# A gated MLP with LoRA adapters on one NeuronCore: the LoRA matmuls of gate and up by two sequences of 128 columns instead of four of 256

## The chip, the core and the metric

One NeuronCore of a Trainium2 chip runs the whole program. The metric is the device time of one execution in microseconds (us); lower is better. Differences between two kernels are told from runs on the same chip.

## What is computed

The input `x` is 64 sequences of 64 tokens with 512 features, all float32. Sequence b uses adapter `idx[b]`, one of 8, with rank 16. The reference, cut to what matters:

```python
def _lora_linear(x, W, A, B, adapter_indices):
    base = jnp.einsum('bsd,df->bsf', x, W)
    Ai = A[adapter_indices]; Bi = B[adapter_indices]
    lora = jnp.einsum('bsr,brf->bsf', jnp.einsum('bsd,bdr->bsr', x, Ai), Bi)
    return base + lora
gate = _lora_linear(x, Wg, Ag, Bg, adapter_indices)        # 512 -> 2048
up = _lora_linear(x, Wu, Au, Bu, adapter_indices)          # 512 -> 2048
h = jax.nn.silu(gate) * up
x = x + _lora_linear(h, Wd, Ad, Bd, adapter_indices)       # 2048 -> 512
x = x + einsum('bct,bcd->bdt', x, weights[adapter_indices])  # 64 x 64 mix of the tokens
```

## The kernel before

float32 products are made of `float32r` matmuls: each operand is split into a high part (a copy into float32r, on ScalarE: `hi`) and a low part (the value minus its high part, on VectorE: `lo`), and high x high, high x low and low x high are summed in PSUM.

**First phase: gate and up.** `GROUPS` = 4 groups of 1024 tokens (16 sequences, `SLOTS`), and in each 16 chunks c of 128 hidden features: 64 steps s. A step computes gate and up of one chunk with seven Strassen-like products (`prod`, L850 to L859, six matmuls of 512 columns each) into PSUM banks RA, RB, RC. The LoRA parts are added into the same banks by four calls of `lora` (L861 to L870) in a step. VectorE and ScalarE combine the banks (`keep_p1`, `make_c11`, `make_u3` and so on), apply the silu, and `store_h` writes h to DRAM. They also split the weights of the next step (`w_hi_raw`, `w_add`, `w_lo_sum`), and near the end of a group the inputs of the next one (`x_add`, `x_hi`, `x_lo`).

**The LoRA of gate and up.** `lora_a` (L873) computes t = x A in plain float32 for four sequences (a quad, 256 columns): the 128 rows of the result are gate and up (2) x four sequences x rank 16. Its stationary operand `aq` is put together on GpSimd by `gather_a`, one copy for each sequence. `t_mask` (VectorE) copies the bank to `t_f` and sets the rows of other sequences to zero; `t_hi` (ScalarE) and `t_lo` (VectorE) write high and low part of gate's t into rows 0 to 63 and 64 to 127 of `t_st[0]`, and of up's t into `t_st[1]`. B, split into high and low by `b_hi` and `b_lo`, is written to DRAM in 8 pieces of two chunks (`store_b`, one DMA), and `gather_b` fetches for each piece and each of the 16 sequences its adapter's rows, twice (rows 0 to 63 and again 64 to 127 of `bq`): 32 DMAs of 64 KB for two steps, all issued by SyncE. `lora` then does for each of two quads a matmul with B's high part and one with its low part: four matmuls of 256 columns in a call, 16 in a step, 1024 in all.

**Order of the work.** It is written out by hand, as one instruction stream for each engine, with semaphores between them. SyncE issues at step s: `load_w(s+2)`, `store_b(s)` for s below 8, half a gather, `store_h(s-1)`, and at c = 2 `load_x` of the next group. In group 0 the pieces of B are split one in each step (`b_hi(s)`, `b_lo(s)` after the second `w_lo_sum`), so a gather can only begin when the piece of its step is stored. TensorE does all of group 0's `lora_a` within step 0, and that of group g+1 in steps 4 to 7 of group g, one quad at the end of each; `t_mask`, `t_hi` and `t_lo` follow in steps 5 to 8. On VectorE `t_mask` stands ahead of `make_c11` and `t_lo` behind it, ahead of `make_u3`, for whose result TensorE waits ahead of the last product of a step (`prod(..., A22, ...)`).

**Second phase: down, and the mixing of tokens.** 16 pairs of 256 tokens; `down` (L955), `turn`, `lora_down`, `mix_tile`. Nothing of it changes.

## Time and profile before

| | us |
|---|---|
| median of 3 runs (1327.96 to 1330.48) | 1329.66 |
| the profiled execution: its time | 1330.62 |
| the profiled execution: its span in the trace | 1328.7 |
| first phase, to about | 862 |

All durations below are of the profiled execution. PE is TensorE's matmuls, PEld its weight loads, DVE VectorE, ACT ScalarE, POOL GpSimd, SP SyncE; SPq is SyncE's issuing of DMAs. The profile's matmuls overlap: one matmul's record reaches over the start of the next, so what a matmul costs in a stream is read from one start to the next, not from its duration.

### The profile page before, as it was taken

How to read it: one execution, taken by the hardware profiler on the slowest of the kernel's cores; microseconds unless marked ns; L12 is line 12 of the kernel's file. 1: busy time of each engine (PE TensorE's matmuls, PEld its weight loads, DVE VectorE, ACT ScalarE, POOL GpSimd, SP SyncE). 2: the span in 40 equal slices, each digit the busy share in tenths (PEclk: the TensorE clock that was granted, in tenths of full speed). 3: DMA queues.
4: the chain of work that ended last, by engine and by line, in shares of the span. 5: the costliest groups of instructions: out<-in, count | busy, mean ns of one | idle time of the engine just before them, and what ended most of it. 6: DMA issues, size and time to landing. Idle time of an engine off the chain costs nothing.

```text
span 1328.7 us, 22783 instructions
## 1 busy us (share of the span) xinstructions
PE 1226.5 (92%) x7072; PEld 1079.6 (81%) x7072; DVE 754.1 (57%) x1341; ACT 500.7 (38%) x951; POOL 96.3 (7%) x190
## 2 busy tenths in 40 slices
PE   3766999989999989999989999989999999999995
PEld 2555778878888878888878888889998999999994
DVE  5434666776666776666776677544334443434341
ACT  3323444454444454444444444443232232322320
POOL 2100110000110000100000000011111111111110
PEclk9778999999999999999989999989999999999998
DMA  3346776567665576665565777375454554455520
GB/s 137 104 145 227 202 211 185 148 196 229 186 168 156 153 206 211 185 176 152 156 201 167 207 209 214 100 235 179 143 149 150 158 162 145 140 156 165 155 62 32
DMA packets 114362, 221.31 MB, mean 167 GB/s; under 512 B 26434, under 2 KB 68546, under 8 KB 114242
## 3 DMA queue, kind: packets, MB, share of 16 engines
q1 hardware_dynamic: 105824, 198.28, 51.2%
q0 software_dynamic: 7552, 19.93, 4.7%
q10 hardware_dynamic: 866, 1.66, 0.3%
q8 instruction: 56, 0.92, 0.3%
q14 instruction: 64, 0.52, 0.1%
HBM read 173.62 MB, written 46.14 MB: 165 GB/s over the span
## 4 chain that ended last, share of the span: by engine, by line
PE 77%; SPq 7%; DVE 5%; issue 4%; ACT 3%; DMA 3%; POOL 0%; ACTq 0%; DVEq 0%
PE ps L856 14%; PE ps L857 14%; PE ps L858 13%; PE ps L868 8%; PE ps L967 5%; PE ps L971 4%; SPq L194 4%; PE ps L975 4%; PE ps L976 4%; PE ps L974 4%; PE ps L969 4%; PE ps L1001 2%; PE ps L885 1%; ACT hh L359 1%; ACT xo_hi L359 1%
## 5 line engine op out<-in xcount | busy, mean ns | idle before, releaser
L856 PE MATMUL ps<-xo_hi,w_hi 128*128 128x512 f32 x896 | 361.2, 403 | 29.0 <-DVE v L657 13.4
L857 PE MATMUL ps<-xo_lo,w_hi 128*128 128x512 f32 x896 | 356.3, 398 | 0.0
L858 PE MATMUL ps<-xo_hi,w_lo 128*128 128x512 f32 x896 | 353.4, 394 | 0.0
L856 PEld LDWEIGHTS ps<-xo_hi,w_hi 128*128 128x128 f32 x896 | 172.2, 192 | 62.0 <-DVE v L657 16.1
L858 PEld LDWEIGHTS ps<-xo_hi,w_lo 128*128 128x128 f32 x896 | 171.2, 191 | 38.4
L868 PEld LDWEIGHTS ps<-t_st,bq 128*128 128x128 f32 x1024 | 158.6, 192 | 53.1 <-DMA bq<-b_dram 32.9
L577 DVE TENSOR_TENSOR hl<-h_raw,hh 128x1024 fp32r<-128x1024 f32 x64 | 78.4, 1226 | 203.1 <-ACT hh L359 203.1
L857 PEld LDWEIGHTS ps<-xo_lo,w_hi 128*128 128x128 f32 x896 | 172.3, 192 | 26.4
L868 PE MATMUL ps<-t_st,bq 128*128 128x256 f32 x1024 | 165.4, 285 | 30.3 <-DMA bq<-b_dram 30.3
L967 PE MATMUL ps<-wd_hl,hh 128*128 128x320 f32 x512 | 167.8, 328 | 6.8 <-DVE hl L577 4.1
L577 DVE TENSOR_TENSOR w_lo<-wsum,w_hi 128x512 fp32r<-128x512 f32 x128 | 88.6, 692 | 145.7 <-ACT w_hi L359 145.7
L971 PE MATMUL ps<-wd_hl,hl 128*128 128x288 f32 x512 | 151.9, 297 | 0.0
L359 ACT ACTIVATE hh<-h_raw 128x1024 fp32r<-128x1024 f32 x64 | 67.6, 1056 | 214.9 <-PE ps L976 208.1
L975 PE MATMUL ps<-wd_hl,hh 128*128 128x256 f32 x512 | 145.1, 283 | 0.0
L976 PE MATMUL ps<-wd_hl,hl 128*128 128x256 f32 x512 | 144.8, 283 | 0.0
L974 PE MATMUL ps<-wd_hl,hh 128*128 128x256 f32 x512 | 144.6, 283 | 0.0
L969 PE MATMUL ps<-wd_hl,hh 128*128 128x256 f32 x512 | 144.4, 282 | 0.0
L967 PEld LDWEIGHTS ps<-wd_hl,hh 128*128 128x128 f32 x512 | 97.9, 191 | 11.0 <-issue 6.5
L969 PEld LDWEIGHTS ps<-wd_hl,hh 128*128 128x128 f32 x512 | 97.7, 191 | 3.6 <-issue 3.6
L974 PEld LDWEIGHTS ps<-wd_hl,hh 128*128 128x128 f32 x512 | 97.6, 191 | 0.0
L976 PEld LDWEIGHTS ps<-wd_hl,hl 128*128 128x128 f32 x512 | 97.3, 190 | 0.0
L971 PEld LDWEIGHTS ps<-wd_hl,hl 128*128 128x128 f32 x512 | 97.1, 190 | 0.0
(65 smaller groups left out, 1434.9 us busy)
## 6 DMA issues: line engine op xcount, KB each, us to landing
bq<-b_dram SPq DMA_DIRECT2D x1024, 64.0 KB, 2.2
raw<-packed SPq DMA_DIRECT2D x64, 512.0 KB, 5.2
h_dram<-h_f SPq DMA_DIRECT2D x64, 512.0 KB, 3.6
h_raw<-h_dram SPq DMA_DIRECT2D x64, 512.0 KB, 4.0
ad_raw<-a_d SPq DMA_DIRECT2D x64, 128.0 KB, 2.7
xs<-x POOLq DMA_DIRECT2D x16, 512.0 KB, 5.0
y_out_dram<-ys POOLq DMA_DIRECT2D x32, 256.0 KB, 3.3
xst<-xg SPq DMA_DIRECT2D x14, 512.0 KB, 6.3
```

What stands on the lines that cost most here:

```text
L359: return act.activation(dst, src, ACT.Copy)
L577: return dve.tensor_tensor(dst, src, hi.bitcast(F32), ALU.subtract)
L856: pe.matmul(bank, st[0], mv[0], start=start and kk == 0, stop=False, skip_group_check=True)
L857: pe.matmul(bank, st[0], mv[1], start=False, stop=False, skip_group_check=True)
L858: m = pe.matmul(bank, st[1], mv[0], start=False, stop=kk == 1, skip_group_check=True)
L868: m = pe.matmul(bank[:, i * QT:(i + 1) * QT], b[:, q, c % PIECE, a:a + P], t_st[u][g % 2][:, q * QT:(q + 1) * QT], start=start and part == ...
L967: pe.matmul(tile[:, 0:HD + 2 * TR], h_hi, w[:, wide[0]:wide[0] + HD + 2 * TR], start=first, stop=False, skip_group_check=True)
L969: pe.matmul(tile[:, plain:plain + HD], h_hi, w[:, LO0:LO0 + HD], start=False, stop=False, skip_group_check=True)
L971: pe.matmul(tile[:, narrow[1]:narrow[1] + HD + TR], h_lo, w[:, narrow[0]:narrow[0] + HD + TR], start=False, stop=False, skip_group_check=True)
L974: pe.matmul(second, h_hi, w[:, HI1:HI1 + HD], start=first, stop=False, skip_group_check=True)
L975: pe.matmul(second, h_hi, w[:, LO1:LO1 + HD], start=False, stop=False, skip_group_check=True)
L976: m = pe.matmul(second, h_lo, w[:, HI1:HI1 + HD], start=False, stop=False, skip_group_check=True)
```

## The change

Eight duos of two sequences (128 columns) take the place of four quads. The four combinations of high and low lie in the 128 rows of one matmul: `bq` has B's high part in rows 0 to 63 and its low part in rows 64 to 127, each with two sequences of 32 rows; every rank row stands twice, and `t_st` has t's high part in the even rows and its low part in the odd ones. So `lora` does one matmul of 128 columns for each of four duos in a call: again 16 in a step and 1024 in all. `lora_a` computes the doubled rows itself (`aq` holds each column twice, its 128 columns are gate and up x two sequences x 16 x 2), in eight duos of 128 columns, at the ends of steps 6 to 13. For a set of four duos (512 columns) `t_mask` makes two masked copies (one signed, one of the low rows), `t_hi` one high part, `t_sum` adds them for gate and for up (64 rows each), and `t_copy` copies them to the other 64 rows. `store_b` writes each piece with four DMAs.

```diff
@@ tiles
-        bq = [... [P, QUADS, PIECE, BC], F32R) ...]
+        bq = [... [P, DUOS, PIECE, WB], F32R) ...]
-        aq = at("aq", 200704, [P, KT * 2, QS, RANK])
+        aq = at("aq", 200704, [P, KT * 2, 2, ROWS])
@@ SyncE: store_b, gather_b
-                sp.dma_start(b_dram[k].rearrange("a r c -> (a r) c"),
-                             b_hl[:, :, :].bitcast(F32).rearrange("p k c -> p (k c)")).then_inc(b_stored, 16)
+                for part in range(2):
+                    for copy in range(2):
+                        sp.dma_start(b_dram[k, part, :, :, copy, :].rearrange("a r (k c) -> (a r) k c", k=PIECE),
+                                     b_hl[:, :, part * WB:(part + 1) * WB].bitcast(F32)).then_inc(b_stored, 16)
...
-                    for half in range(2):
-                        r = half * QR + (b % QS) * RANK
-                        sp.dma_start(bq[n % 2][r:r + RANK, b // QS, :, :]..., b_dram[k, bass.ds(a, 1)]...)
+                    for part in range(2):
+                        r = (part * 2 + b % 2) * ROWS
+                        sp.dma_start(bq[n % 2][r:r + ROWS, b // 2, :, :]..., b_dram[k, part, bass.ds(a, 1)]...)
@@ GpSimd: gather_a
-                    pool.wait_ge(t_done, g * QUADS + q)
-                for s in range(QS):
-                    a = number(pool, g * SLOTS + q * QS + s)
-                    pool.tensor_copy(aq[:, :, s, :], a_all[:, bass.ds(a, 1), :, :]...)
+                    pool.wait_ge(t_done, g * DUOS + q)
+                for k in range(2):
+                    a = number(pool, g * SLOTS + q * 2 + k)
+                    src = a_all[:, bass.ds(a, 1), :, :].rearrange("p a k r -> p (a k) r")
+                    pool.tensor_copy(aq[:, :, k, :].rearrange("p k (r d) -> p k r d", d=2),
+                                     src.unsqueeze(3).to_broadcast([P, KT * 2, RANK, 2])).then_inc(a_gathered, 1)
@@ ScalarE: t_hi is one copy of 128 x 512; new:
+            def t_copy(g, b):
+                ...
+                for u in range(2):
+                    act.wait_ge(t_set, 2 * i + u + 1)
+                    t = t_st[u][g % 2]
+                    a, z = (slice(0, 2 * ROWS), slice(2 * ROWS, P))[::1 - 2 * u]
+                    hi(t[z, cols], t[a, cols].bitcast(F32)).then_inc(t_ready, 1)
@@ ScalarE, step 0: for b in 0, 1
+                t_hi(0, b)
+                x_hi(0, 3 + 2 * b)
+                t_copy(0, b)
+                x_hi(0, 4 + 2 * b)
@@ ScalarE and VectorE, in the loop over the steps
-                if 5 <= c < 9 and g + 1 < GROUPS:
-                    t_mask(g + 1, c - 5)          # t_hi(g + 1, c - 5) on ScalarE
+                if c in (10, 14) and g + 1 < GROUPS:
+                    t_mask(g + 1, c // 14)        # t_hi and t_copy(g + 1, c // 14) on ScalarE
...
                 make_c11(s)
-                if 5 <= c < 9 and g + 1 < GROUPS:
-                    t_lo(g + 1, c - 5)
+                if c in (10, 14) and g + 1 < GROUPS:
+                    t_sum(g + 1, c // 14)
@@ VectorE: new bodies
+                for dst, m in ((t_f[:, :], sign_mask), (t_low[g][:, 0:HALF], low_mask)):
+                    dve.tensor_tensor(dst..., bank, m[:, :].unsqueeze(2).to_broadcast([P, SLOTS // 2, SEQ]), ALU.mult)
...
+                for u in range(2):      # t_sum
+                    r = slice(u * 2 * ROWS, (u + 1) * 2 * ROWS)
+                    dve.tensor_tensor(t_st[u][g % 2][r, cols], t_low[g][r, 0:HALF], t_hi_s[g][r, 0:HALF].bitcast(F32),
+                                      ALU.add).then_inc(t_set, 1)
@@ VectorE, step 0: for b in 0, 1
+                t_mask(0, b)
+                if b == 0:
+                    x_add(0, 3, None)
+                x_lo(0, 3 + 2 * b)
+                t_sum(0, b)
+                x_lo(0, 4 + 2 * b)
@@ TensorE: lora
-                for part in range(2):
-                    for i in range(2):
-                        q = pair * 2 + i
-                        a = part * WB + u * P
-                        m = pe.matmul(bank[:, i * QT:(i + 1) * QT], b[:, q, c % PIECE, a:a + P],
-                                      t_st[u][g % 2][:, q * QT:(q + 1) * QT], ...)
+                for i in range(SD):
+                    q = half * SD + i
+                    m = pe.matmul(bank[:, i * DT:(i + 1) * DT], b[:, q, c % PIECE, u * P:(u + 1) * P],
+                                  t_st[u][g % 2][:, q * DT:(q + 1) * DT], ...)
@@ TensorE: when step 0 of a group may use t, and when lora_a runs
-                    pe.wait_ge(t_lo_done, 2 * QUADS * (g + 1))
+                    pe.wait_ge(t_ready, 2 * SETS * (g + 1))
...
-                if 4 <= c < 8 and g + 1 < GROUPS:
-                    lora_a(g + 1, c - 4)
+                if 6 <= c < 14 and g + 1 < GROUPS:
+                    lora_a(g + 1, c - 6)
```

## Rows read from the trace of the kernel before

**Rows 1.** The page: busy time and share of an engine, then the chain's shares.

```profile
PE 1226.5 (92%) x7072; PEld 1079.6 (81%) x7072; DVE 754.1 (57%) x1341; ACT 500.7 (38%) x951; POOL 96.3 (7%) x190
...
PE 77%; SPq 7%; DVE 5%; issue 4%; ACT 3%; DMA 3%; POOL 0%; ACTq 0%; DVEq 0%
```

**Rows 2.** Busy time by stretch: one undisturbed step, 11.5 us long.

```profile
436.90:448.40 11.50, 11.50 (x61) 9.78 (x60) 8.23 (x15) 4.94 (x8) 0.00 (x0) 1.00 0.76 219
```

**Rows 3.** Groups of instructions by shape: busy us, mean ns, idle before.

```profile
L868 PE MATMUL ps<-t_st,bq 128*128 128x256 f32 x1024 | 165.4, 285 | 30.3 <-DMA bq<-b_dram 30.3
...
L885 PE MATMUL ps<-xst,aq 128*128 128x256 f32 x128 | 35.3, 425 | 12.1 <-POOL aq L288 12.1
```

**Rows 4.** Timeline of TensorE: start us, us, instruction; a `lora` call in its stream.

```profile
442.84 0.64 PE L868 MATMUL ps<-t_st,bq 128*128 128x256 f32 x4
443.31 0.40 PE L856 MATMUL ps<-xo_hi,w_hi 128*128 128x512 f32 x1
```

**Rows 5.** Timeline of TensorE: matmuls of 128 columns, and what follows them.

```profile
902.36 0.31 PE L984 MATMUL ps<-eye_r,td_hl 128*96 128x128 f32 x2
902.51 0.36 PE L967 MATMUL ps<-wd_hl,hh 128*128 128x320 f32 x1
902.71 0.28 PE L969 MATMUL ps<-wd_hl,hh 128*128 128x256 f32 x1
```

**Rows 6.** Timeline of the weight loads in the same stretch.

```profile
902.45 0.19 PEld L967 LDWEIGHTS ps<-wd_hl,hh 128*128 128x128 f32 x1
902.56 0.19 PEld L969 LDWEIGHTS ps<-wd_hl,hh 128*128 128x128 f32 x1
```

**Rows 7.** Timeline of the weight loads: two of 128 columns after a pause.

```profile
873.05 0.19 PEld L967 LDWEIGHTS ps<-wd_hl,hh 128*128 128x128 f32 x1 [0.52 <-DVE hl L577]
873.16 0.19 PEld L969 LDWEIGHTS ps<-wd_hl,hh 128*128 128x128 f32 x1
```

**Rows 8.** Timeline of step 0: `lora_a`, its copies, and the first `lora`.

```profile
20.89 2.35 PE L885 MATMUL ps<-xst,aq 128*128 128x256 f32 x8
...
34.12 3.78 PE L885 MATMUL ps<-xst,aq 128*128 128x256 f32 x8 [3.90 <-POOL aq L288]
...
38.64 0.30 POOL L288 COPY aq<-a_all 128x128 f32 x1 [4.57 <-PE ps L885]
...
41.80 3.78 PE L885 MATMUL ps<-xst,aq 128*128 128x256 f32 x8 [3.90 <-POOL aq L288]
...
49.96 1.22 PE L868 MATMUL ps<-t_st,bq 128*128 128x256 f32 x4 [4.38 <-DMA bq<-b_dram]
```

**Rows 9.** Chain of work between 60 and 190 us: start us, us, what.

```profile
68.89 2.63 DMA b_dram<-b_hl
...
87.00 2.08 DMA bq<-b_dram
...
118.89 5.79 DMA bq<-b_dram
...
152.31 2.10 DMA bq<-b_dram
```

**Rows 10.** SyncE: `load_x`'s four issues; what `gather_b` executes, ns min/median/max.

```profile
107.50 2.47 SPq L166 DMA_DIRECT2D xst<-xg  x4
...
L194 SPq DMA_DIRECT2D bq<-b_dram x159: 315/368/1440, 71.7 to 199.6; - x159
L194 SPq FUSED_REGOPS  x80: 37/37/42, 71.5 to 199.5; - x80
```

**Rows 11.** Timeline of VectorE in step 13 of group 1, and TensorE's last product.

```profile
442.83 0.69 DVE L577 TENSOR_TENSOR w_lo<-wsum,w_hi 128x512 fp32r<-128x512 f32 x1 [1.17 <-ACT w_hi L359]
443.44 0.69 DVE L588 TENSOR_TENSOR xst<-xst,xst 128x512 f32<-128x512 f32 x1
...
444.90 0.69 DVE L657 TENSOR_TENSOR v<-ps,p_s 128x512 f32<-128x512 f32 x1 [0.17 <-PE ps L858]
...
446.53 0.40 PE L856 MATMUL ps<-xo_hi,w_hi 128*128 128x512 f32 x1
```

More of the change, by code:

```diff
@@ L21 @@
 SLOTS = GT // SEQ
-QUADS, QS = 4, 4
-QT, QR = QS * SEQ, QS * RANK
+DUOS, DT = 8, 2 * SEQ
+SETS, SD = 2, DUOS // 2
+QS = 4
 BLK = 2 * HALF
@@ L319, in _ @@
             pool.wait_ge(a_in, 16)
-            for q in range(QUADS):
+            for q in range(DUOS):
                 gather_a(0, q)
@@ L323, in _ @@
             gather_a(1, 0)
-            for k in range(2, 6):
+            for k in range(2, PIECES):
                 load_b(k)
-            gather_a(1, 1)
-            load_b(6)
-            gather_a(1, 2)
-            load_b(7)
-            gather_a(1, 3)
-            for g in range(2, GROUPS):
-                for q in range(QUADS):
+            for g in range(1, GROUPS):
+                for q in range(g == 1, DUOS):
                     gather_a(g, q)
@@ L502, in _ @@
             w_hi_sum(0, 1)
-            for q in range(QUADS):
-                t_hi(0, q)
-                x_hi(0, 3 + q)
-            act.wait_ge(const_in, 48)
+            for b in range(SETS):
+                t_hi(0, b)
+                x_hi(0, 3 + 2 * b)
+                t_copy(0, b)
+                x_hi(0, 4 + 2 * b)
+            act.wait_ge(const_in, 64)
             hi(eye_r[:, :], eye_f[:, :])
@@ L533, in _ @@
                     b_hi(s)
-                if 5 <= c < 9 and g + 1 < GROUPS:
-                    t_hi(g + 1, c - 5)
+                if c in (10, 14) and g + 1 < GROUPS:
+                    t_hi(g + 1, c // 14)
+                    t_copy(g + 1, c // 14)
                 silu_1(s)
@@ L751, in _ @@
             w_lo_sum(0, 1)
-            dve.wait_ge(const_in, 48)
-            for q in range(QUADS):
-                t_mask(0, q)
-                if q == 0:
+            dve.wait_ge(const_in, 64)
+            for b in range(SETS):
+                t_mask(0, b)
+                if b == 0:
                     x_add(0, 3, None)
-                t_lo(0, q)
-                x_lo(0, 3 + q)
+                x_lo(0, 3 + 2 * b)
+                t_sum(0, b)
+                x_lo(0, 4 + 2 * b)
             for s in range(STEPS):
@@ L859, in prod, with lora @@
                 return m
-            def lora(bank, s, u, pair, start):
+            def lora(bank, s, u, half, start):
                 g, c = divmod(s, CH)
                 b = bq[(s // PIECE) % 2]
-                for part in range(2):
-                    for i in range(2):
-                        q = pair * 2 + i
-                        a = part * WB + u * P
-                        m = pe.matmul(bank[:, i * QT:(i + 1) * QT], b[:, q, c % PIECE, a:a + P],
-                                      t_st[u][g % 2][:, q * QT:(q + 1) * QT], start=start and part == i == 0,
-                                      stop=part == i == 1, skip_group_check=True)
+                for i in range(SD):
+                    q = half * SD + i
+                    m = pe.matmul(bank[:, i * DT:(i + 1) * DT], b[:, q, c % PIECE, u * P:(u + 1) * P],
+                                  t_st[u][g % 2][:, q * DT:(q + 1) * DT], start=start and i == 0,
+                                  stop=i == SD - 1, skip_group_check=True)
                 return m
             def lora_a(g, q):
-                i = g * QUADS + q
-                pe.wait_ge(a_gathered, QS * (i + 1))
+                i = g * DUOS + q
+                pe.wait_ge(a_gathered, 2 * (i + 1))
                 if q == 0:
@@ L910, in step @@
                 if s == 0:
-                    for q in range(QUADS):
+                    for q in range(DUOS):
                         lora_a(0, q)
@@ L1060, in by_chunk @@
         return np.asarray(b).reshape(ADAPTERS * RANK, PIECES, PIECE, P)
+    rows = np.arange(P)[:, None]
+    own = rows % (2 * ROWS) // ROWS == np.arange(SLOTS // 2)[None, :] % 2
+    low = rows % 2 == 1
     arrays = {
@@ L1075 @@
         "w1": ar(np.asarray(L1_cond_weights)),
-        "slot_mask": (np.arange(P)[:, None] % QR // RANK == np.arange(QS)[None, :]).astype(np.float32),
+        "slot_mask": ar(np.stack([own * np.where(low, -1.0, 1.0), own * low]).astype(np.float32)),
         "tok_mask": (np.arange(P)[:, None] // SEQ == np.arange(TR)[None, :] // RANK).astype(np.float32),
```

95 lines of the change are left out of this document (50 added, 45 removed).

## The prediction

> **What bounds the kernel now.** I read the shares of the page first. TensorE is busy for 92% of the span and holds 77% of the chain; VectorE has 57% of its own time [rows 1]. Then a stretch of one undisturbed step: TensorE is never idle in its 11.5 us, VectorE works 8.2 us of it, ScalarE 4.9 [rows 2]. So in steady state a nanosecond less of matmul is a nanosecond less of time, as long as VectorE's 3.3 us of slack last. Group 0 is different: in the chain between 60 and 190 us stand the store of a piece of B, SyncE's issues and the landing of `bq` [rows 9], and `lora` waited 30.3 us for `bq` in all [rows 3]. There nothing that TensorE saves counts, and whatever lengthens the way from `b_lo` through `store_b` and `gather_b` does.
>
> I work against the profiled execution's own 1330.6 us (span 1328.7 and 1.9 around it). It lies 0.9 us above the median of the runs shown; I take that off at the end.
>
> **1. The `lora` matmuls: 1024 of 256 columns become 1024 of 128.** What does one cost? Four of 256 take 443.31 - 442.84 = 0.47 us from the first start to the next line's, 118 ns each [rows 4]. Halved columns would give some 60 ns if columns set the pace. But each matmul has its own stationary operand of 128 columns, and the number of weight loads does not change. How long does a load hold its port? After a pause, with nothing ahead to wait for, the second load starts 873.16 - 873.05 = 0.11 us after the first [rows 7]. The trace has one place with short matmuls, the pairs `turn` (128 columns moving, 96 of weights). Behind them the loads for L967 and L969 start at 902.45 and 902.56, again 0.11 apart [rows 6]. And the time is really lost: from the first of the pair to L969 it is 902.71 - 902.36 = 0.35 us [rows 5]. If columns set it, two of 128 would take 0.06 each and the one of 320 columns 0.15, together 0.27; with loads that hold the port for 0.08 (96 columns) and 0.11 (128) it is 0.08 + 0.11 + 0.15 = 0.34, which fits. So a matmul of 128 columns behind a load of 128 columns costs about 0.11 us. I take 111 ns, hence 7 ns less than now for each: 1024 x 0.007 = 7.2 us gained. Bounds: 0 (118 ns as now) and 1024 x 0.058 = 59 us (60 ns).
>
> [...]
>
> **2. `lora_a`.** 32 matmul halves of 256 columns in a group (128 instructions in all [rows 3]) become 64 of 128. They are plain float32, 3.78 us for eight at the low clock, 0.43 us apart [rows 8], and half of that, 0.215, at the high one; half the columns take half again, and 0.11 us is just what a weight load allows. So TensorE's time for them stays: 0 us. Bounds: 0 and, if a float32 weight load were twice as slow, +6.9 us a group outside step 0, three times; I keep that as tail.
>
> **3. Step 0: the chain of duos.** `lora_a` and `gather_a` take turns there, since there is one `aq`. Now: 0.74 us from the end of a quad (34.12 + 3.78 = 37.90) to the first copy (38.64), then the other three copies until 41.80, then 3.78 us of matmuls: 7.7 us four times from 20.89 on [rows 8]. After: two copies in place of four, but each of twice the elements and eight turns instead of four. [...] Seven turns of 3.0 to 3.9 us, mostly at the low clock, from 22.5 on: the last duo is done at about 48.7 (46 to 51.5), against 45.6 now. Behind it stands more than before: a mask of 512 columns (0.69), `t_hi` (0.62), then in both streams the work on `x`: `x_hi(0,5)` 1.06 and `x_lo(0,5)` 1.23, then two sums of 0.69 and the last `t_copy` 0.62: 5.6 us, where now the mask and the split took 1.9. `t_ready` comes at about 54.3. Now the first `lora` starts at 49.96, when `bq` lands [rows 8]; `bq` will land at 51.5 to 53. So +4.4 us (bounds +1.5, where `bq` alone decides, and +7.5).
>
> **4. Group 0: storing and fetching B.** A store is one DMA now, 2.63 us from issue to the next step of the chain [rows 9]. It becomes four. Four DMAs in a row on SyncE took 2.47 us, 0.6 each, single ones 0.37 [rows 10]; three more cost 1.2 to 1.9 us, I take 1.5. [...] In the chain, the pieces for steps 2 and 3 count: `store_b(1)` ahead of the gather for step 2 (+1.5), `store_b(2)` and `store_b(3)` ahead of that for step 4, where SyncE never waited (+3.0), and `store_b(5)` and `store_b(7)` ahead of those for steps 6 and 8 (+1.5 each; the stores of steps 4 and 6 fall into waits of SyncE of over 2.5 us). Together +7.5 us (bounds 5 and 9.5). The fetch stays at 32 DMAs of 64 KB with 32 runs of 2 KB instead of 16 of 4 KB. One address calculation now serves two DMAs: 80 for 160 [rows 10]. The two will read from different parts, so there may be one for each: 16 more of 0.08 us, 1.3 us in each of the first two gathers of the chain and half of it in the next two, 3.9 us. I take 2 of it (0 to 3.9). What hides them now is nothing: TensorE waits there anyway. From step 10 on SyncE has slack, 32 issues of 0.5 us in 23 us.
>
> **5. VectorE in steps 10 and 14.** Now mask and split of a quad are short and lie in steps 5 to 8. In step 13 VectorE runs `w_lo_sum` at 442.83, `x_add` 443.44, `make_c11`, and `make_u3` from 444.90 to 445.59; TensorE needs it at 446.53, so there is 0.9 us of slack, and 0.6 us for each instruction of this size [rows 11]. Steps 10 and 14 have an `x_add` too, and get two masks ahead and two sums behind `make_c11`: `make_u3` starts at 442.83 + 7 x 0.605 = 447.07 in that step's times, is done at 447.76 and TensorE resumes 1.3 us late. Behind it wait `make_c22`, `make_c12`, silu and h, shifted by as much as TensorE itself. Two such steps in three groups: +7.8 us (bounds 4 and 10, the upper with a bit more at step 15, where `x_lo` already fills VectorE). The stalls that go are those of step 8, which takes 12.0 us in group 1 where 11.5 is usual: 0.4 us three times, -1.2. ScalarE's part is 3.7 us a group against 3.4, in its 6 us of slack.
>
> **Sum.** 1330.6 - 7.2 + 4.4 + 7.5 + 2 + 7.8 - 1.2 = 1343.9; less 0.9 for the median: **1343.0 us**, 1.0% slower.
>
> **Rivals.**
> *Columns set the pace (faster).* The load is hidden behind the matmul ahead at any length and a `lora` matmul takes 60 ns: 59 us in place of 7.2, less what falls into waits (3): 1294. For it: in a stream of 256 columns the loads cost nothing visible [rows 4]. Against: rows 5 to 7. It decides the sign as soon as a matmul takes less than about 98 ns (118 less 20 us over 1024). Chance 0.08.
> *A load holds the port 0.085 us only*, as the 96 columns do behind a short matmul [rows 5]: 1024 x 0.033 = 34 us, so 1343.0 - 26.6 = 1316. [...] Chance 0.06.
> *The costs hide and it comes out even.* Stores go out at 0.4 and no address calculation is added (+5), `bq` decides step 0 (+1.5), VectorE catches up (+2), and the matmuls go to 108 ns (-10): 1328 to 1332. Chance 0.07.
> *The long side*: calculations for every DMA, copies slowed by VectorE in step 0, one more stall at the ends of groups: 1343 + 2 + 3 + 2 + 3 to 1353 and up. It is the forecast's upper end; beyond 1356 I give 0.06.
> The forecast's own case, 1333 to 1356, holds 0.73.
>
> The range that leaves out two in ten: 1330 to 1357. A difference of 0.2%, 2.7 us, is about what can be told from none: faster 0.15, the same 0.07, slower 0.78.
>
> **What would show it.** The distance from start to start within a `lora` call: 0.11 us if I am right, 0.06 if columns set it. An undisturbed step of 11.4 us in place of 11.5. The first `lora` at about 54 us, and waiting for ScalarE's copy rather than for `bq`. Waits for `bq` ahead of steps 2, 4, 6 and 8 still there. Two steps of each of the first three groups with TensorE waiting over 1 us for `make_u3`. The prediction is wrong if a `lora` matmul takes less than 98 ns, or if `store_b`'s four DMAs do not lengthen the chain of group 0 and steps 10 and 14 show no stall.

## The result, and the profile after

The changed kernel takes **1357.38 us** (median of 4 runs, 1356.88 to 1358.11), the kernel before 1329.68 beside it: ratio 1.0214, 95% interval 1.0202 to 1.0226, so 27 to 30 us slower. Forecast were 1343.0 us and 1330 to 1357. The sign was right; the loss is twice the 13 us forecast, just outside the range.

The page of the kernel after, against [rows 1]: the same engines work about as long, the span is 27.8 us longer. (Its chain view breaks off half way, with 37% for TensorE, so I don't read it.)

```profile
span 1356.5 us, 23547 instructions
PE 1220.7 (90%) x7200; PEld 1081.4 (80%) x7200; DVE 759.2 (56%) x1325; ACT 501.1 (37%) x943; POOL 97.2 (7%) x190
...
DMA packets 138448, 225.57 MB, mean 166 GB/s; under 512 B 26962, under 2 KB 77266, under 8 KB 138322
```

Busy time can't tell where the rest went, so next the waits of TensorE and of its weight loads: line, what it waited for, us in total, times, longest. Against [rows 3], where `bq` held it for 30.3 us, it is 44.2. The wait for v (`make_u3`) was 13.4 us in 6 places and is 22.6 in 12.

```profile
PE ps L888 <- DMA bq<-b_dram: 44.2, 6, 17.0
...
PEld ps L878 <- DVE v L678: 24.3, 12, 3.4
...
L878 PE MATMUL ps<-xo_hi,w_hi 128*128 128x512 f32 x896 | 371.3, 414 | 38.5 <-DVE v L678 22.6
```

Where in the span? I compare the starts of the first `lora` matmul of each piece of B, read from TensorE's timeline, and the end of group 0:

| | step 0 | 2 | 4 | 6 | 8 | last h of group 0 |
|---|---|---|---|---|---|---|
| before, us | 49.96 | 89.12 | 124.73 | 154.45 | 183.09 | 278.2 |
| after, us | 56.32 | 99.05 | 137.16 | 169.53 | 202.32 | 307.7 |
| difference | +6.4 | +9.9 | +12.4 | +15.1 | +19.2 | +29.5 |

The whole loss arises in group 0. At the last h of groups 1, 2 and 3 the difference is 30.8, 30.4 and 28.3 us: later groups win by the matmuls about what they lose to VectorE. The step from +19.2 to +29.5 can be read off the lengths of the steps in the trace: six duos of 0.89 us in steps 8 to 13 (the quads before stood in steps 4 to 7) are 5.3, the two steps with a wait for v 3.3, and a granted clock of 0.50 for 6.8 us, from 202.1 on, behind the wait of step 8 makes that step 3.2 us longer; less 1.3 by the shorter matmuls and 0.4 for the old stall in step 8.

An undisturbed step of the kernel after is 11.36 us, against [rows 2] 11.5, with TensorE never idle (columns as there):

```profile
590.00:601.36 11.36, 11.36 (x64) 9.83 (x63) 7.04 (x12) 4.94 (x8) 0.73 (x2) 1.00 0.65 198
```

TensorE around a `lora` call, then step 10 of group 2, its wait in brackets:

```profile
631.53 0.56 PE L888 MATMUL ps<-t_st,bq 128*128 128x128 f32 x4
631.93 0.45 PE L878 MATMUL ps<-xo_hi,w_hi 128*128 128x512 f32 x1
632.21 0.40 PE L879 MATMUL ps<-xo_lo,w_hi 128*128 128x512 f32 x1
...
634.72 0.56 PE L888 MATMUL ps<-t_st,bq 128*128 128x128 f32 x4
636.70 0.50 PE L878 MATMUL ps<-xo_hi,w_hi 128*128 128x512 f32 x1 [1.43 <-DVE v L678]
```

The call seems to cost 0.40 us for four, but the matmul behind it is followed after 0.28 where 0.227 is usual: 0.40 + 0.05, some 112 ns each. Within the call the second start comes only 57 ns after the first and the others 113 and 110 ns apart, so the records of the first and of the matmul behind the call seem to begin early, and starts must be read over the whole call and one matmul more. Read so, the kernel before has 120 ns, not 118. The cause of the wait is in VectorE's timeline of the same step, all its instructions from 631 to 636.7:

```profile
631.52 0.69 DVE L593 TENSOR_TENSOR w_lo<-wsum,w_hi 128x512 fp32r<-128x512 f32 x1 [1.13 <-ACT w_hi L365]
632.13 0.68 DVE L654 TENSOR_TENSOR t_f<-ps,sign_mask 128x512 f32<-128x512 f32 x1
632.73 0.68 DVE L654 TENSOR_TENSOR t_low<-ps,low_mask 128x512 f32<-128x512 f32 x1
633.33 0.68 DVE L604 TENSOR_TENSOR xst<-xst,xst 128x512 f32<-128x512 f32 x1
633.93 0.68 DVE L671 TENSOR_TENSOR p_s<-ps,p_s 128x512 f32<-128x512 f32 x1
634.53 1.39 DVE L665 TENSOR_TENSOR t_st<-t_low,t_hi_s 64x512 fp32r<-64x512 f32 x2
635.96 0.69 DVE L678 TENSOR_TENSOR v<-ps,p_s 128x512 f32<-128x512 f32 x1
```

Seven instructions back to back and then `make_u3`, without a pause: just the queue that the forecast counted. Behind a wait of 1.43 us, step 10 and step 14 of a group are each 1.66 us longer than their neighbours (13.91 for 12.25, 13.02 for 11.36).

SyncE's issues in group 0, start and length; against [rows 9], where the store's step in the chain took 2.63 us:

```profile
74.99 1.96 SPq L186 DMA_DIRECT2D b_dram<-b_hl  x4
81.19 16.20 SPq L203 DMA_DIRECT2D bq<-b_dram  x32
```

From the first store to the first fetch it is 6.20 us; before it was 2.78 at this place. Of these, 1.96 are the four issues and 4.2 the rest of the landing. By the DMA queues' records a store was 512 KB in 128 packets of 4 KB (166 ns each, 1.3 us for each of the 16 DMA engines) and is 1 MB in 1024 packets of 1 KB (47 ns each, 3.0 us for each). At later pieces, where SyncE does not wait for the landing, the distance was 0.6 to 0.7 us and is 2.2 to 3.3.

The queues' records show a second thing. GpSimd's `load_b`, which loads the raw next piece of B (256 KB in 64 packets), waits for the same `b_lo` as the store and is issued 0.27 us after its first DMA, then as now:

```profile
69.16 0.54 POOL L293 DMA_DIRECT2D b_raw<-b_gu  x1 [19.73 <-DVE b_hl L577]
```
```profile
75.26 0.54 POOL L303 DMA_DIRECT2D b_raw<-b_gu  x1 [22.86 <-DVE b_hl L593]
```

Before, the store's packets lay at 69.73 to 71.18 us, and the first of `load_b` began at 71.15, when they were through. Now the store's lie at 75.90 to 80.68, and all 64 of `load_b` (327 ns each, 1.3 us for each DMA engine) fall inside, at 76.97 to 78.76, where few of the store's move. So of the 3.3 us by which the store's packets take longer, 1.7 are its own and about 1.3 go to `load_b`. No run moves `load_b` out of the way, so what that alone would give back is not shown.

Step 0: GpSimd's copies of `aq` and the first `lora`, against [rows 8]:

```profile
34.27 0.40 POOL L298 COPY aq<-a_all 128x256 f32 x1 [2.85 <-PE ps L905]
34.94 1.40 POOL L298 COPY aq<-a_all 128x256 f32 x1 [0.27 <-issue]
...
48.53 2.08 PE L905 MATMUL ps<-xst,aq 128*128 128x128 f32 x8 [1.84 <-POOL aq L298]
...
54.12 1.40 DVE L665 TENSOR_TENSOR t_st<-t_st_f,t_st 64x512 fp32r<-64x512 f32 x2
54.83 1.35 ACT L365 ACTIVATE t_st<-t_st 64x512 fp32r<-64x512 f32 x2 [1.89 <-DVE t_st L665]
...
56.32 1.09 PE L888 MATMUL ps<-t_st,bq 128*128 128x128 f32 x4 [5.72 <-ACT t_st L365]
```

`lora` waits for the last `t_copy`, no longer for `bq`.

### The profile page after: what moved, and what is told of

It reads as the page before. It is cut to its first block and busy times, and to the rows that moved or that the text cites. A ratio compares the mean times of both kernels' runs of the same rounds, so it can differ in the third digit from the quotient of the medians.

```text
span 1356.5 us, 23547 instructions
## 1 busy us (share of the span) xinstructions
PE 1220.7 (90%) x7200; PEld 1081.4 (80%) x7200; DVE 759.2 (56%) x1325; ACT 501.1 (37%) x943; POOL 97.2 (7%) x190
## 3 DMA queue, kind: packets, MB, share of 16 engines
q1 hardware_dynamic: 129760, 202.47, 50.6%
q10 hardware_dynamic: 1010, 1.66, 0.3%
## 5 line engine op out<-in xcount | busy, mean ns | idle before, releaser
L878 PE MATMUL ps<-xo_hi,w_hi 128*128 128x512 f32 x896 | 371.3, 414 | 38.5 <-DVE v L678 22.6
L888 PE MATMUL ps<-t_st,bq 128*128 128x128 f32 x1024 | 146.7, 266 | 49.9 <-DMA bq<-b_dram 44.2
L987 PEld LDWEIGHTS ps<-wd_hl,hh 128*128 128x128 f32 x512 | 97.6, 191 | 10.1 <-issue 6.4
L989 PEld LDWEIGHTS ps<-wd_hl,hh 128*128 128x128 f32 x512 | 97.3, 190 | 3.6 <-issue 3.6
L994 PEld LDWEIGHTS ps<-wd_hl,hh 128*128 128x128 f32 x512 | 97.4, 190 | 0.0
L996 PEld LDWEIGHTS ps<-wd_hl,hl 128*128 128x128 f32 x512 | 97.1, 190 | 0.0
L995 PEld LDWEIGHTS ps<-wd_hl,hh 128*128 128x128 f32 x512 | 96.8, 189 | 0.0
```

Source lines behind the costliest of these rows:

```text
L878: pe.matmul(bank, st[0], mv[0], start=start and kk == 0, stop=False, skip_group_check=True)
L888: m = pe.matmul(bank[:, i * DT:(i + 1) * DT], b[:, q, c % PIECE, u * P:(u + 1) * P], t_st[u][g % 2][:, q * DT:(q + 1) * DT], start=start a ...
L987: pe.matmul(tile[:, 0:HD + 2 * TR], h_hi, w[:, wide[0]:wide[0] + HD + 2 * TR], start=first, stop=False, skip_group_check=True)
L989: pe.matmul(tile[:, plain:plain + HD], h_hi, w[:, LO0:LO0 + HD], start=False, stop=False, skip_group_check=True)
L994: pe.matmul(second, h_hi, w[:, HI1:HI1 + HD], start=first, stop=False, skip_group_check=True)
L995: pe.matmul(second, h_hi, w[:, LO1:LO1 + HD], start=False, stop=False, skip_group_check=True)
```

## The experiments

Each number is the median, then the ratio to the kernel before, run beside it, with its 95% interval. "Loss" is that ratio less 1, times 1329 us; the kernel after has 28.4 by this measure.

**1. Before, with `lora` moving 128 columns** and the same 1024 loads (each matmul covers one half of its quad's columns, so half of the LoRA product of gate and up is left out).

```diff
-                        m = pe.matmul(bank[:, i * QT:(i + 1) * QT], b[:, q, c % PIECE, a:a + P],
-                                      t_st[u][g % 2][:, q * QT:(q + 1) * QT], ...
+                        h = (2 * i + part) * QT // 2
+                        m = pe.matmul(bank[:, h:h + QT // 2], b[:, q, c % PIECE, a:a + P],
+                                      t_st[u][g % 2][:, pair * 2 * QT + h:...+ QT // 2], ...
```

> The kernel before, with one edit: each of the 1024 LoRA matmuls moves 128 columns instead of 256 (high part for one half of the columns, low part for the other, so half of the LoRA product is left out); weight loads, order, DMAs and everything else stay. It prices the changed matmul by itself. Theory: the load of 128 weight columns sets the pace, 108 to 112 ns from start to start, so a step goes from 11.52 to 11.36 us and the kernel gains 8 to 10 us (about 1321 us). Rival: the columns set it (60 ns), a step of 10.6 us and a gain of 50 to 59 us, and the loss of the changed kernel outside the matmuls would be 80 us. Second rival, 85 ns: gain 30 us.

1319.83 us, 0.9932 [0.9916, 0.9949]: 9 us gained (7 to 11), 9 ns for each of 1024 matmuls. With half the columns they are only 7% shorter: the load sets the pace. This settles both faster rivals.

**2. Before, with four stores a piece** (two of them of the same parts to memory that nobody reads: the bytes of the kernel after).

```diff
+                for part in range(2):
+                    cols = slice(part * WB, (part + 1) * WB)
+                    sp.dma_start(rows[:, :, cols], b_hl[:, :, cols]...).then_inc(b_stored, 16)
+                    sp.dma_start(b_more[k, part]..., b_hl[:, :, cols]...).then_inc(b_stored, 16)
```

> The kernel before, with one edit: each piece of B is stored by four DMAs of 256 KB (two of them to memory that nothing reads) instead of one of 512 KB, and the gather waits for all four. Theory: in the changed kernel the four intervals between the lora calls of steps 0, 2, 4, 6 and 8 grew by 3.6, 2.5, 2.6 and 4.1 us, mostly by the stores: more issues on SyncE and a later landing (6.2 us from the first issue to the first gather where it was 2.7), and by the clock, which stays low after the longer waits of steps 6 and 8. So +11 to +14 us (1341 to 1344 us), first gather of piece 1 at 6 us after the first store, waits for bq at steps 6 and 8 of 4 to 5 us instead of 1.6. Rival: stores cost their issues alone, as predicted: +1.5, +3, +1.5, +1.5 us, 7.5 in all (1337 us). Rival 2: they are hidden and the growth came from the other edits: below +3 us.

1349.06 us, 1.0147 [1.0130, 1.0164]: 19.5 us lost (17 to 22), more than expected. The stores alone are the larger part of the loss. In the trace:

```profile
70.06 0.60 SPq L181 DMA_DIRECT2D b_dram<-b_hl  x1
70.70 0.62 SPq L182 DMA_DIRECT2D b_more<-b_hl  x1
71.36 0.63 SPq L181 DMA_DIRECT2D b_dram<-b_hl  x1
72.04 0.63 SPq L182 DMA_DIRECT2D b_more<-b_hl  x1
76.10 15.61 SPq L199 DMA_DIRECT2D bq<-b_dram  x32
```

First store to fetch is 6.04 us, nearly as in the kernel after (6.20); `lora` resumes at 52.06, 93.52, 133.01, 166.81 and 200.57 us, 17.5 later than before at step 8. The records of the queues show `load_b` inside the store here too (72.29 to 73.54 us in 71.31 to 75.59), and the granted clock is 0.50 for 6.8 us from 165.3 and again from 199.4, so the 19.5 are the price of the stores with all that follows from them.

**3. After, with one store a piece**; the fetch reads each row twice through a source with a step of 0.

```diff
-                                     b_dram[k, part, bass.ds(a, 1)].rearrange("a r d c -> (a r d) c"))\
+                                     src.unsqueeze(1).to_broadcast([RANK, 2, PIECE * WB]))\
```

> The changed kernel, with one edit: each piece of B is stored once, by one DMA of 4 KB rows, and the gather reads every row twice (a source step of zero) in place of reading doubled rows. Bytes and runs that arrive in bq are the same, 32 DMAs of 64 KB. Theory: the store chain goes back to 2.7 us, and the waits for bq at steps 2, 4, 6 and 8 shrink by 3 us each or more, and with the shorter waits of steps 6 and 8 less of them runs at the low clock: 12 to 17 us faster than the changed kernel (1340 to 1345 us). Rival, issues alone as predicted: 7.5 us faster (1350 us). If reading with a step of zero makes the gather slower, SyncE's 16 issues take more than 8.1 us and the landing more than 2 us; then the gain is smaller and says nothing of the stores.

1493.26 us, 1.1247 [1.1209, 1.1284]. The edit brought a cost of its own. Issues of the fetch in this trace (ns min/median/max), then in that of the kernel after:

```profile
L202 SPq DMA_DIRECT2D bq<-b_dram x1024: 562/562/1544, 32.1 to 1000.4; - x171
```
```profile
L203 SPq DMA_DIRECT2D bq<-b_dram x1024: 315/316/1777, 34.2 to 864.3; - x171
```

With what lies between, a fetch goes out each 0.75 us instead of 0.5, 32 of them take 24 us, more than the two steps that use them, and SyncE sets the pace in every group. The time says nothing about the stores; the next experiment asks again. But one row of this trace bears on them: in the otherwise changed kernel, one store of 512 KB lets the fetch begin 2.82 us after it, as before, and `load_b` begins when it is through (78.86 us, the store's last packet 78.87).

```profile
76.58 0.35 SPq L184 DMA_DIRECT2D b_dram<-b_hl  x1
79.40 24.08 SPq L202 DMA_DIRECT2D bq<-b_dram  x32
```

**5. After, with two stores of 512 KB a piece** in 4 KB rows: half the issues, the same 1 MB.

```diff
-                for part in range(2):
-                    for copy in range(2):
-                        sp.dma_start(b_dram[k, part, :, :, copy, :]..., b_hl[:, :, part * WB:(part + 1) * WB]...
+                for copy in range(2):
+                    sp.dma_start(b_dram[k, :, :, copy, :, :]..., b_hl[:, :, :, :]...
```

> The changed kernel, with one edit: each piece of B is stored by two DMAs of 512 KB in rows of 4 KB (one for each of the doubled rows) instead of four of 256 KB in runs of 1 KB; bytes written are the same 1 MB, the gather's 32 DMAs read runs of 2 KB as before. Four stores cost the kernel before 19.6 us. Theory: it is the number of issues (0.5 to 0.75 us each on SyncE, which is the bound of group 0) and the late landing of the many 1 KB runs: from the first store to the first gather 3.2 to 4 us instead of 6.2, and 12 to 15 us faster than the changed kernel (1342 to 1345 us). Rival: it is the doubled bytes, which fill the DMA queues: first gather after 5 us or more, gain below 6 us.

1352.6 us, 1.0181 [1.0152, 1.0210]: some 4 us back, where 12 to 15 were expected; the rival holds.

```profile
73.99 0.82 SPq L185 DMA_DIRECT2D b_dram<-b_hl  x2
79.99 16.18 SPq L202 DMA_DIRECT2D bq<-b_dram  x32
```

The issues take 0.82 us instead of 1.96, and yet the fetch begins 6.00 us after the first store. So at the first pieces the doubled bytes set the landing (with `load_b` inside it here too, at 76.92 to 78.71 us), not the number of issues or the packet size; the later ones, where SyncE does not wait for the landing (1.1 to 2.2 us now), gain by fewer issues.

**4. After, with dummy matmuls (24 and 18) ahead of the waits of steps 6 and 8**, so that TensorE has work there.

```diff
+                fill = {6: 24, 8: 18}.get(s, 0)
+                for i in range(fill):
+                    pe.matmul(RD, w_hi[s % 2][:, 0:P], xo_hi[0][:, 0:HALF], ...)
```

> The changed kernel, with one edit: ahead of the wait for bq at step 6 TensorE does 24 matmuls of 512 columns and ahead of that at step 8 another 18, into the bank that the next LoRA call overwrites (5.5 and 4.1 us of waits of 8.1 and 6.0 us). [...] Rival: the time behind these waits hangs on the other engines or the gathers, not on the matmuls' speed: same time within 1 us.

1356.12 us, 1.0201 [1.0184, 1.0218], 1.7 us under the loss of the kernel after, where I had expected 5 to 6: a small part at most. The kernel after has a granted clock of 0.50 for 10.2 us from 164.5 and 6.8 us from 202.1; 5.2 and 6.6 us of that lie behind the waits for `bq`, in work, and half of them was my estimate. The kernel before has a granted clock of 1.00 at these places. With the dummies 3.4 us at 0.50 are left, from 171.7. From `lora` of step 6 to that of step 8 it is 32.6 us with them and 32.8 without: what TensorE loses there at 0.50 it waits off at the next piece. Behind step 8 no piece is waited for any more, and that step takes 12.4 us in place of 15.5. The dummies themselves cost some 0.5 us ahead of step 6.

**6. After, with `t_sum` behind `make_c22`** and `t_copy` behind the second silu.

```diff
-                if c in (10, 14) and g + 1 < GROUPS:      (ahead of make_u3, ahead of the second silu)
-                    t_sum(g + 1, c // 14)                 ... t_copy(g + 1, c // 14)
+                if c in (10, 14) and g + 1 < GROUPS:      (behind make_c22, behind the second silu)
+                    t_sum(g + 1, c // 14)                 ... t_copy(g + 1, c // 14)
```

> The changed kernel, with one edit: in steps 10 and 14 of a group VectorE does the two sums (t_sum) behind make_c22 instead of ahead of make_u3, and ScalarE the copies (t_copy) after its second silu. Theory (as predicted): the 1.5 us stalls ahead of the last product in steps 10 and 14 come of four more instructions of 0.6 us ahead of make_u3 against 0.9 us of slack; with two of them moved behind it 1.2 us of each goes, six times: 7 us faster than the changed kernel (1350.5 us), stalls of 0.3 us left. Rival: VectorE is full in these steps anyway, what is moved delays make_c12, silu and h, and TensorE waits at the next step's second product instead: gain below 3 us.

1359.43 us, 1.0241 [1.0218, 1.0265]: not faster, where 7 us were expected. Step 10 loses 1.2 us less, but behind step 14 stands step 15, full already, where TensorE now waits:

```profile
292.42 0.50 PE L879 MATMUL ps<-xo_hi,w_hi 128*128 128x512 f32 x1 [2.06 <-ACT p_s L413]
```

By the steps' lengths the work is too much for steps 14 and 15 together: what step 14 gains, step 15 loses and more.

**7. After, with eight stationary operands in step 0**, so that `gather_a` waits for no duo.

```diff
+        aq_0 = [at(f"aq_0{q}", 163840 + q * 2048, [P, KT * 2, 2, ROWS]) for q in range(DUOS)]
-                if g + q:
+                if g > 1 or g and q:
```

> The changed kernel, with one edit: in group 0 each of the eight duos has its own stationary operand (in space that the second bq buffer uses later), so GpSimd's copies no longer wait for TensorE and all eight lora_a run one after the other. Theory: the chain of turns sets the first lora call (56.3 us after the start against 50.0 before); without it the last duo is done before 35 us, and the first lora call waits for bq, which lands at about 52: 4 to 5 us faster than the changed kernel (1353 us). Rival: step 0 has no hold on the rest, since the next gather hangs on other work: same time within 1 us.

1353.3 us, 1.0189 [1.0162, 1.0215]: 3.3 us back by the ratio, 4.1 by the medians. The first `lora` waits for `bq` and nothing else:

```profile
52.31 1.11 PE L890 MATMUL ps<-t_st,bq 128*128 128x128 f32 x4 [24.24 <-DMA bq<-b_dram]
```

56.32 - 52.31 = 4.0 us is what the turns cost; the other 2.35 of the 6.4 is the later `bq`, behind four stores.

**8. After, with `lora_a` two steps earlier** (steps 4 to 11, masks in 8 and 12).

```diff
-                if 6 <= c < 14 and g + 1 < GROUPS:
-                    lora_a(g + 1, c - 6)
+                if 4 <= c < 12 and g + 1 < GROUPS:
+                    lora_a(g + 1, c - 4)
```

> The changed kernel, with one edit: lora_a of the next group stands at the ends of steps 4 to 11 instead of 6 to 13, and masks, sums and copies in steps 8 and 12 instead of 10 and 14. Theory: in group 0 TensorE waits 8.1 and 6.0 us for bq at steps 6 and 8, and a duo at the end of step 5 or 7 (0.9 us) costs nothing, while one after step 8 costs its whole time; two of eight duos move from after step 8 into these places or ahead of them, of which one lies in a wait and one delays the next piece: 1 to 2 us faster than the changed kernel, no more (1355.5 us). Rival: the old place of lora_a was worth its 6.9 us in group 0, since all of it lay beside the waits: 3.5 us or more faster.

1355.54 us, 1.0209 [1.0190, 1.0229]: 0.7 us by the ratio, which is not told from none. The expected 1 to 2 us lie within the interval.

**15. Before, with four more VectorE instructions in each of steps 10 and 14.**

```diff
+                    for dst in (b_raw[:, :, :], b_hl[:, :, WB:2 * WB]):      # ahead of and behind make_c11
+                        dve.tensor_tensor(dst, src, src, ALU.add).then_inc(filled, 1)
```

> The kernel before, with one edit: in steps 10 and 14 of groups 0 to 2 VectorE does two more instructions of 128x512 ahead of make_c11 and two behind it, ahead of make_u3, on data that nothing uses; nothing else is added. It prices the place and amount of the changed kernel's masks and sums. Theory: make_u3 comes 2.4 us later against 0.9 us of slack, 1.5 us of stall in each of six steps: +8 to +10 us (about 1338 us). Rival: the next steps' slack gives it back: +3 us or less.

1336.43 us, 1.0062 [1.0037, 1.0086]: 8.2 us lost (5 to 11). The six steps are 1.36 us longer each, 8.2 in all (1.66 in the kernel after). VectorE's share stands by itself, without the rest of the change.

**9. Duos with B stored once.** From the kernel before: the doubled rows lie as (rank, high or low), so one store of 512 KB and one source serve both halves of `bq`; the mask, `t_hi` and `t_lo` go by two duos in steps 6, 8, 10 and 12, `t_lo` behind `make_c22`; step 0 has its own operands.

```diff
-                         r = half * QR + (b % QS) * RANK
-                         sp.dma_start(bq[n % 2][r:r + RANK, ...], b_dram[k, bass.ds(a, 1)].rearrange("a r c -> (a r) c"))
+                         r = half * QR + (b % 2) * ROWS
+                         sp.dma_start(bq[n % 2][r:r + ROWS, ...], b_dram[k, bass.ds(a, 1)].rearrange("a r (q c) -> (a r q) c", q=2))
```

> The duos with the kernel before's stores: the rows of bq are (rank, part of B) for t high and again for t low, so B is stored once, in one DMA of 4 KB rows, and the gather reads the same 64 KB for both halves with one address calculation; t keeps the mask, hi and lo of the kernel before, for two duos (256 columns) at a time, in steps 6, 8, 10 and 12, with lo behind make_c22; in group 0 each duo has its own stationary operand; lora_a stands in steps 4 to 11. Theory: what made the changed kernel slower was the doubled stores in group 0 (19.6 us by themselves), VectorE's longer work in steps 10 and 14 and step 0's turns; without them the matmuls' 9.5 us remain, less 1.7 for lora_a work that no longer lies in a wait of group 0: 7 to 9 us faster than the kernel before (about 1320 us), intervals between the lora calls of steps 0 to 8 within 1 us of before, no stall over 0.5 us in steps 6 to 14. Rival: the duos cost something that these edits don't touch (more matmul starts in lora_a, 2 KB runs in the gather): same time as before or slower.

1320.46 us, 0.9938 [0.9924, 0.9951]: 8.2 us faster than before. The idea, freed from its three costs, pays what the shorter matmuls give in experiment 1.

**14. The same with four stores** (two to memory that nobody reads, as in 2).

```diff
-                sp.dma_start(b_dram[k]..., b_hl[:, :, :, :]...).then_inc(b_stored, 16)
+                for dst in (b_dram, b_more):
+                    for q in range(2):
+                        rows = dst[k].rearrange("a r (q k c) -> (a r) q k c", q=2, k=PIECE)
+                        sp.dma_start(rows[:, q, :, :], b_hl[:, q, :, :].bitcast(F32)).then_inc(b_stored, 16)
```

> The kernel with duos and one store (1320.5 us), with one edit: each piece is stored by four DMAs of 256 KB, half of them to memory that nothing reads, 1 MB in all as in the changed kernel, and the gather waits for all four. Theory: the stores' price does not hang on the kernel around them: +16 to +20 us as on the kernel before (1337 to 1341 us), so with the duos too it is the stores that turn a gain into a loss. Rival: on the kernel before they were dear because of something that the duos change (one address calculation, lora_a's place): below +10 us.

1337.3 us, 1.0054 [1.0036, 1.0072]: by the ratios 15.4 us above the duo, just under the 16 to 20 expected. The stores' price again, in a kernel with the new matmuls.

**10. Before, with each piece of B split and stored a step earlier.** The diff shows VectorE's part; ScalarE's `b_hi`, SyncE's `store_b(1)` and the second fetch move with it.

```diff
-                if 0 < s < PIECES:
-                    b_lo(s)
+                if 0 < s < PIECES - 1:
+                    b_lo(s + 1)
```

> The kernel before, with one edit: piece 1 of B is split and stored in step 0 and pieces 2 to 7 one step earlier, so that SyncE never waits for the split of a piece, and the gather for step 2 is issued in step 0. It takes away the place in which the stores hurt. Theory: group 0 is bound by the way from the split through the store to the gather; without it the waits for bq at steps 2, 4, 6 and 8 (13.5, 10.7, 1.7 and 1.6 us, 27.5 in all) go but for some 3 us at step 4: 22 to 28 us faster (about 1304 us). Rival: SyncE's own issues (16 us for each gather, and x and h beside them) are the bound, and the waits only move: less than 12 us faster.

1312.2 us, 0.9871 [0.9854, 0.9888], 17 us faster, where 22 or more was expected. All waits for `bq` after step 0 are gone, but VectorE now stands in step 3, since `b_hi(4)` must wait until the store of piece 3, issued at 93.62 us (right behind `load_x`'s four, 90.34 to 92.88), has landed before it overwrites `b_hl`:

```profile
102.71 0.63 ACT L360 ACTIVATE b_hl<-b_raw 128x512 fp32r<-128x512 f32 x1 [8.73 <-DMA b_dram<-b_hl]
103.37 0.69 DVE L579 TENSOR_TENSOR b_hl<-b_raw,b_hl 128x512 fp32r<-128x512 f32 x1 [8.66 <-ACT b_hl L360]
...
105.32 0.80 PE L859 MATMUL ps<-xo_hi,w_hi 128*128 128x512 f32 x1 [7.44 <-DVE v L659]
```

**13. After, with the pieces a step earlier** and its four stores.

```diff
-                    b_lo(s)
+                    b_lo(s + 1)
```

> The changed kernel, with the one edit that took the waits for bq from the kernel before (1312.2 us): piece 1 of B is split and stored in step 0, pieces 2 to 7 one step earlier. The four stores stay. Theory: the 27.7 us are 19.6 of stores, which cost only because group 0 hangs on them, 4 of step 0's turns and 9 of VectorE's stalls in steps 10 and 14, less 9.5 of matmuls and 1 of old stalls; off the chain the stores cost nothing, and what is left against the kernel before with the same edit is 4 + 9 - 9.5 - 1 = +2 to +4 us: 1314 to 1317 us. Rival: the doubled stores also cost bandwidth and issues beside the chain, then 1325 us or more.

1327.13 us, 0.9986 [0.9972, 1.0001]: 30 us faster than the kernel after, but 15 slower than 10; 2 to 4 was forecast for the case that the stores cost only in the chain. The same wait is longer here:

```profile
114.81 0.63 ACT L366 ACTIVATE b_hl<-b_raw 128x512 fp32r<-128x512 f32 x1 [10.69 <-DMA b_dram<-b_hl]
115.47 0.69 DVE L595 TENSOR_TENSOR b_hl<-b_raw,b_hl 128x512 fp32r<-128x512 f32 x1 [10.63 <-ACT b_hl L366]
...
117.42 0.79 PE L881 MATMUL ps<-xo_hi,w_hi 128*128 128x512 f32 x1 [9.52 <-DVE v L680]
```

At the end of group 0 it is 12.7 us behind experiment 10: 6.3 from step 0, 3.3 from steps 10 and 14, and 3.1 left. TensorE's waits between step 0 and the end of step 7 are 3.1 us longer than in 10 (the one above by 2.1). The 2.6 us that the shorter matmuls should win in 16 steps do not show; behind step 0 the granted clock is 0.50 for 17 us here and for 10 us in experiment 10. So the stores seem to keep a part of their price even here, on another path; no experiment takes it out.

**11 and 12. The duo of 9 with the pieces a step earlier, and with SyncE reading the 16 adapter numbers before its first fetch, while it waits for the first store.**

```diff
-                    b_lo(s)
+                    b_lo(s + 1)
...
+                    sp.wait_ge(t_done, DUOS)            # SyncE, ahead of the second fetch
...
+            for b in range(SLOTS):                      # 12 alone
+                slot_numbers[b] = number(sp, b)
```

> The run with duos and one store, and beside that B's pieces a step earlier as in the kernel with that edit alone. Theory: the two edits touch different bounds (TensorE's matmuls in steady state, the store and gather chain in group 0), so their gains add, and where nothing waits for bq any more lora_a's place costs nothing: 9 to 11 us faster than the kernel with the earlier pieces alone, about 1295 us. Rival: with the waits gone, group 0 is bound by SyncE or VectorE, and the matmuls' gain is lost there: 6 us or less.

> As the run before (duos, one store, pieces a step earlier), with one more edit: SyncE reads the 16 adapter numbers of group 0 while it waits for the first piece, not between the first store and the first gather (now 22.6 to 32.3 us). Theory: the first gather begins when the first store has landed, about 25 us, the first lora call at 43 instead of 50 us, and as t is done at about 35 us all of it is gained: 6 to 7 us (about 1289 us). Rival: t, or x's splits on ScalarE and VectorE, come later than 43 us: less than 3 us.

1295.69 us, 0.9766 [0.9746, 0.9785], and 1292.2, 0.9724 [0.9708, 0.9739]. The first is 16.5 us faster than 10 by the medians and 14 by the ratios, more than the 9 to 11 expected. Part of it is experiment 10's own: its step 2 takes 16.04 us, with a wait of 2.73 for ScalarE, and only 11.45 in 11. The rest is not taken apart. In the second the first `lora` starts at 43.56 us, 7.2 earlier than in 11; the gain on 11 is 3.5 us by the medians and 5.6 by the ratios, where 6 to 7 was expected. It is the best version, 37 us faster than the kernel before and 65 than the kernel after.

## Why the prediction came out half as large as the loss

1. **The `lora` matmuls: right.** 111 ns forecast, some 112 in the trace (110 to 113 from start to start behind the first), 0.16 us for an undisturbed step (11.52 to 11.36), -9 us in experiment 1 for -7.2. What was a little off is the 118 ns of the kernel before, 120 over one matmul more. The rivals of 60 and 85 ns fell.

2. **`lora_a`: right in TensorE's time** (111 ns from start to start, 215 for half as many before). What I did not see is its place. Before, the quads of steps 5 and 7 lay in part beside waits for `bq` in group 0, and cost little there; the duos come in steps 8 to 13 too, at their full 0.89 us (12.25 us for a step with one, 11.36 without). I put this at 2 to 3 us in group 0, which is an estimate: experiment 8, in which steps 4 and 5 have a duo and 12 and 13 none, gave 0.7 us, not told from none.

3. **Step 0: somewhat low.** +4.4 forecast, +6.4 measured: the last duo was done at 50.6 us where I had 48.7, since six of the seven turns took 3.9 to 4.9 us, at a granted clock of 0.50 from 24.6 to 62.1 us (one copy was 1.40 us instead of 0.40, beside `x_add` on VectorE). My 3.0 to 3.9 us for a turn were an estimate, and no run shows the 3.0: the shortest of the seven, the first, took 3.65. The chain behind it took 5.6 us, as forecast. My mechanism, copies rather than `bq`, held, and experiment 7 gives it 4.0 us; had those copies gone, the later `bq` would still have cost 2.35.

4. **The stores: the step that failed.** I took the landing's time as unchanged, an assumption that no run shows, and it was wrong. I counted issues but not bytes: 1 MB must land instead of 512 KB, and where SyncE waits for the landing the fetch begins 6.2 to 6.3 us after the first store in place of 2.8 (2.82 in experiment 3, with 512 KB). Nor did I see that a longer store runs into `load_b`, about 1.3 of these us. With that, the term of 7.5 (bounds 5 and 9.5) is 15 to 20 us by experiments 2 and 14, low clock behind the longer waits included. Experiment 5 shows that it is mostly bytes at the first pieces and issues at the later ones. The term was bounded by issue time alone, so its upper end was no bound, and the range inherited the fault.

   From `lora` to `lora` the intervals grew by 3.6, 2.5, 2.7 and 4.2 us, where I had put 1.5, 3.0, 1.5 and 1.5 for the stores. The stores of steps 4 and 6 did fall into waits of SyncE: `store_b(5)` is issued no later after the `lora` of step 4 than before (18.5 us for 19.2), `store_b(7)` 1.1 later. It is `store_b(5)` and `store_b(7)` themselves that cost more, 3.3 and 3.2 us to the fetch for 0.6, with the fetch's own 16 issues. At step 4 a part was hidden: the issues of its fetch ended 6.2 us later, counted from the `lora` of step 2, but the last DMA, which took 5.8 us to land before [rows 9], landed after about 2.

   The address calculations: one for every DMA, as feared, but the issues behind them are 316 ns where every other one was 368 [rows 10], and 16 of them take 8.0 us in place of 7.7. The four fetches of the chain took 0.5 to 0.8 us longer each, 2.7 in all, near the 2 I took.

5. **VectorE in steps 10 and 14: right, a little low.** Waits of 1.3 us were forecast and are 1.43 in all six, but the steps are 1.66 us longer: 10 us for 7.8, at the upper bound; experiment 15 gives 8.2. 3.3 us of them lie in group 0.

**The account.** By the experiments: stores 15 to 20 (the 2.35 us in step 0 included), turns of step 0 4, VectorE 8 to 10, `lora` -9, the old stalls -1, the place of `lora_a` 2 to 3, clock 2 to 3, which gives 21 to 30 us against 28 measured. That these parts add up so is argued, not shown: experiment 2 has low clocks behind its longer waits too, so clock and stores overlap in it.

The rival "the long side" had the right size (1353 and up, 0.06 beyond 1356) but mostly not the cause: calculations for every DMA and a copy of 1.40 us beside VectorE's `x_add` came true, one more stall at the ends of groups did not, and the stores' landing is not in it.

## What to carry to other kernels

When a change writes more copies of something that is read back at once, price the landing by its bytes, not only the issues: here 512 KB more in three more DMAs put 3.4 us on a turn of store and fetch where SyncE waits for the landing and 2 to 3 where it does not, and the stores in all cost 15 to 20 us, about twice what the shorter matmuls won. Look also at what else is started by the same event: a transfer that used to run behind the store now ran inside it. Ask first whether the order of the rows in memory can serve both readers (experiment 9), since then the copy is not needed. And where the weight load set the pace, as for `lora` here, fewer columns gained almost nothing: 120 to 112 ns for half of them.

## What the runs showed of the hardware

- In experiment 3 a DMA whose source has three dimensions (a step of 0 inside) took 562 ns to issue on SyncE, against 316 in the kernel after; from one to the next it was 0.75 us against 0.5.
- In step 0 of the kernel after, a GpSimd copy of 128x256 took 0.40 us in 15 of the 16 copies from 22.8 to 52.0 us (128x128 took 0.30 before, [rows 8]) and once 1.40, from 34.94 us, when VectorE's `x_add` (34.87 to 36.09) and `x_lo` ran beside it.
- Writing 512 KB by 4 KB packets occupied each DMA engine for 1.3 us (kernel before); 1 MB took 3.0 us by 1 KB packets (kernel after) and 2.6 by 4 KB ones (experiment 5), so packet size was worth 0.4 us, bytes 1.3.
- A load of 256 KB that GpSimd issued 0.27 us behind a store's first DMA ran after a store of 512 KB (from 71.15 us, the store through at 71.18) and inside one of 1 MB (76.97 to 78.76 in 75.90 to 80.68).
